# Wider spill rows, one fetch per half stack, and score maxima dealt from the third quad on

## What is computed

```
x   = x + layernorm(attention(layernorm(x)))       # q, k, v = x @ W.T + b, 16 heads
x   = x + layernorm(ffn(layernorm(x)))
ffn: xn = norm(x); abel = gelu(xn @ abel_w + b); top 2 of xn @ moe_gate_w
     moe = sum of the two experts, then three rotations; out = x + abel*(1-gate) + moe*gate
```

## Time and profile before

| | |
|---|---|
| median of 3 runs | 1971.94 us (1971.53 to 1973.84) |
| the profiled execution: its time | 1979.73 us |
| the profiled execution: its span | 1977.9 us |
| mean granted TensorE clock | 0.942 |
| PE busy | 1598.2 us, 81% |
| DVE busy | 1217.5 us, 62% |
| ACT busy | 930.2 us, 47% |
| POOL busy | 706.5 us, 36% |
| DMA moved | 241.47 MB, mean 122 GB/s |

### The profile page before, as it was taken

The page is one execution under the profiler, slowest core; times in us unless marked ns, Lnnn a source line. Parts: engine busy times, 40 slices in busy tenths (PEclk is TensorE's granted clock), DMA queues, the critical chain, the costliest instruction groups (busy, mean ns, idle before and its releaser), DMA issues. The chain is left out here.

```text
span 1977.9 us, 33425 instructions
## 1 busy us (share of the span) xinstructions
PE 1598.2 (81%) x10429; PEld 1074.0 (54%) x10430; DVE 1217.5 (62%) x3633; ACT 930.2 (47%) x1788; POOL 706.5 (36%) x716
## 2 busy tenths in 40 slices
PE   3888887888888888888888888849999999999800
PEld 2544444444444444444444444538888888888700
DVE  6756675675775775775765765334565566556367
ACT  1045655755755755755755646412332333233234
POOL 1011223423423423423413413522444444444458
PEclk9899999999999999999999998979999999999955
DMA  3233234234234234234144132574565565565377
GB/s 118 80 108 97 67 108 148 74 121 151 73 124 149 70 124 151 72 123 150 68 127 140 60 121 69 165 219 107 124 140 123 114 143 126 108 140 118 45 264 252
DMA packets 185548, 241.47 MB, mean 122 GB/s; under 512 B 24585, under 2 KB 156049, under 8 KB 185297
## 3 DMA queue, kind: packets, MB, share of 16 engines
q1 hardware_dynamic: 158544, 203.58, 32.6%
q0 software_dynamic: 26880, 36.33, 11.1%
HBM read 133.40 MB, written 105.91 MB: 121 GB/s over the span
## 5 line engine op out<-in xcount | busy, mean ns | idle before, releaser
L952 ACT ACTIVATE pexp<-scT 128x512 f32<-128x512 f32 x768 | 441.8, 601 | 355.1 <-PE scT L739 343.8
L1122 DVE TENSOR_REDUCE mx<-work 128x1 f32<-128x320 f32 (+2 forms) x1024 | 492.8, 549 | 50.6 <-PE work L719 47.7
L1599 POOL DMA_INDIRECT y_rows<-rows_add,row_of x144 | 227.0, 1576 | 295.6 <-DMA y_rows<-rows_add,row_of 225.3
L739 PE MATMUL scT<-w 128*128 128x192 bf16 (+3 forms) x1536 | 275.6, 278 | 54.8 <-ACT pexp L952 53.8
L719 PE MATMUL work<-w 126*128 126x320 bf16 (+4 forms) x1280 | 265.8, 300 | 55.4 <-DVE mx L1122 25.9
L1631 PE MATMUL h_ps<-inT,w1c 128*128 128x256 f32 x1152 | 263.1, 382 | 2.4 <-DVE inT L1683 2.4
L1644 PE MATMUL o_ps<-w,hT 128*128 x1152 | 260.4, 379 | 0.0
L1631 PEld LDWEIGHTS h_ps<-inT,w1c 128*128 128x128 f32 x1152 | 220.4, 192 | 33.5 <-issue 2.9
L739 PEld LDWEIGHTS scT<-w 128*128 128x128 bf16 x1536 | 124.3, 98 | 205.4 <-ACT pexp L952 142.0
L1574 ACT ACTIVATE rows_add<-rows_out,row_share 128x257 f32<-128x257 f32 x144 | 65.9, 506 | 354.6 <-DVE rows_out L1699 266.1
L1644 PEld LDWEIGHTS o_ps<-w,hT 128*128 128x128 f32 x1152 | 213.4, 190 | 26.1
(11 more groups left out here) (173 smaller groups left out, 2176.0 us busy)
## 6 DMA issues: line engine op xcount, KB each, us to landing
w<-split_spill SPq DMA_DIRECT2D x384, 128.0 KB, 3.0
split_spill<-split SPq DMA_DIRECT2D x64, 384.0 KB, 3.2
rows_in<-z_rows SPq DMA_DIRECT2D x72, 265.0 KB, 5.4
y_rows<-pre SPq DMA_DIRECT2D x16, 514.0 KB
y<-y_rows SPq DMA_DIRECT2D x16, 514.0 KB, 6.7
x_rows<-x SPq DMA_DIRECT2D x16, 512.0 KB, 2.6
abel_rows<-pre SPq DMA_DIRECT2D x16, 512.0 KB
abel_in<-abel_rows SPq DMA_DIRECT2D x16, 512.0 KB
```

The source lines that it names most:

```text
L739: ins = nc.tensor.matmul(scT[n % 2][:, at:at + hi - lo], tile(kst[par][0:K_EXP, h, :], t), qst[par][0:K_EXP, h, lo:hi], start=True, stop=True)
L952: nc.scalar.activation(pexp[:, (q * GROUP + n) % NPB, :], scT[n % 2][:, :], ACT.Exp, scale=DH ** -0.5).then_inc(s_exp, 1)
L1122: nc.vector.reduce_max(mx[:, c:c + 1], work[t][:, 0:n], AX_X).then_inc(w_free[t], 1)
L1599: pool.indirect_dma_start(kept.y_rows, bass.IndirectOffsetOnAxis(ap=row_of[n][:, r:r + 1], axis=0), rows_add[n % 2][:, r, :], None, comput ...
```

## The change

The spill gets six slots for each projection in place of three, in the order of the products. `put` issues three DMAs, of three, two and one slot (768 KB in all where it was 384 KB); for k, a part is repeated by a broadcast source. The products are reordered so that this works; they are the same six pairs. `restack` is one DMA of 96 partitions (768 KB) where it was six of 16. On SP `put(2)` comes before `restack(0)`, and the load of x comes behind all fetches, no longer ahead of the first `put`. The maxima go in two DMAs where they went in eight, for which their column is now h * 4 + t. `B_FROM` is 2: the 64 max units go over ten quads, six or seven a quad. On DVE both `values` come ahead of `finish_a(2)`, no longer behind `finish_a(3)`.

```diff
-Q_PART = [0, 0, 1, 1, 0, 2]
-K_PART = [0, 1, 0, 1, 2, 0]
-NGRP = len(Q_PART)
+PRODUCTS = [(0, (0, 1, 2), (0, 0, 0)), (3, (0, 1), (1, 1)), (5, (0,), (2,))]
+NGRP = 6
-B_FROM = 3
+B_FROM = 2
-        spill = nc.dram_tensor("split_spill", [2, 4, P, 3, S], BF16, kind="Internal").ap()
+        spill = nc.dram_tensor("split_spill", [2, 4, P, NGRP, S], BF16, kind="Internal").ap()
...
             def put(b, par, m):
                 sp.wait_ge(s_split, b * 4 + m + 1)
-                sp.dma_start(spill[par, m], split[:, m, :, :]).then_inc(s_spill[m], 16)
+                for at, q_parts, k_parts in PRODUCTS:
+                    n = len(q_parts)
+                    if m % 2:
+                        src = split[:, m, k_parts[0]:k_parts[0] + 1, :].broadcast_to([P, n, S])
+                    else:
+                        src = split[:, m, 0:n, :]
+                    sp.dma_start(spill[par, m][:, at:at + n, :], src).then_inc(s_spill[m], 16)
 
             def restack(b, par, m):
                 half = m // 2
-                st, parts = (kst, K_PART) if m % 2 else (qst, Q_PART)
-                sp.wait_ge(s_spill[m], b * 16 + 16)
-                for g, part in enumerate(parts):
-                    src = spill[par, m].rearrange("(h d) s c -> d h s c", d=DH)[:, :, part, :]
-                    sp.dma_start(st[par][g:MASK_ROW:NGRP, 8 * half:8 * half + 8, :], src)\
-                      .then_inc(s_stack[half], 16)
+                st = kst if m % 2 else qst
+                sp.wait_ge(s_spill[m], (b + 1) * len(PRODUCTS) * 16)
+                src = spill[par, m].rearrange("(h d) g c -> (d g) h c", d=DH)
+                sp.dma_start(st[par][0:MASK_ROW, 8 * half:8 * half + 8, :], src).then_inc(s_stack[half], 16)
...
             def step(s, par, i):
                 if here(s, 0):
-                    if not isinstance(s, int) or s + 2 < B:
-                        sp.wait_ge(s_bn, (s + 1) * NTOK)
-                        sp.wait_ge(s_xn, (s + 1) * NTOK)
-                        plain(sp)
-                        load_x(sp, xin[par], s + 2, s_xin[par])
                     wait(sp, s_sc, (s - 1) * UNITS)
...
                     put(s, par, 0)
                     put(s, par, 1)
+                    put(s, par, 2)
                     restack(s, par, 0)
-                    put(s, par, 2)
-                    restack(s, par, 1)
                     put(s, par, 3)
-                    restack(s, par, 2)
-                    restack(s, par, 3)
+                    for m in range(1, 4):
+                        restack(s, par, m)
+                    if s + 2 < B:
+                        sp.wait_ge(s_bn, (s + 1) * NTOK)
+                        sp.wait_ge(s_xn, (s + 1) * NTOK)
+                        plain(sp)
+                        load_x(sp, xin[par], s + 2, s_xin[par])
...
-                    for t in range(NT):
-                        for part in range(N_MAX):
-                            r = MAX_ROW + part
-                            sp.dma_start(qst[par][r:r + 1, :, t * P:(t + 1) * P],
-                                         mrow[t * HEADS:(t + 1) * HEADS, part, :]).then_inc(s_mrow, 16)
+                    for part in range(N_MAX):
+                        r = MAX_ROW + part
+                        sp.dma_start(qst[par][r:r + 1, :, :].rearrange("o h (t c) -> o (h t) c", c=P),
+                                     mrow[:, part, :]).then_inc(s_mrow, 16)
...
             def maximum(b, h, t):
-                c = t * HEADS + h
+                c = h * NT + t
...
(DVE, step)
+                if proj:
+                    for n in range(2):
+                        values(s, par, n)
                 if finish:
                     finish_a(s - 2, 2)
                 more = not isinstance(s, int) or s + 1 < B
                 if more:
                     stats(s + 1, 1 - par)
                 if finish:
                     finish_a(s - 2, 3)
-                if proj:
-                    for n in range(2):
-                        values(s, par, n)
```

More of the change, by code:

```diff
@@ L713, in max_unit @@
                 if t == 0 and h % 8 == 0:
-                    pe.wait_ge(s_stack[h // 8], (b + 1) * 2 * NGRP * 16)
+                    pe.wait_ge(s_stack[h // 8], (b + 1) * 2 * 16)
                 use(b, t, ("max", h))
@@ L735, in score_unit @@
                 if q == 0 and n == 0:
-                    pe.wait_ge(s_mrow, (b + 1) * NT * N_MAX * 16)
+                    pe.wait_ge(s_mrow, (b + 1) * N_MAX * 16)
                 wait(pe, s_exp, u - 1)
@@ L916, in first_part @@
                 full(act, b, w, "project")
-                wait(act, s_spill[m], b * 16)
+                wait(act, s_spill[m], b * len(PRODUCTS) * 16)
                 nc.scalar.activation(split[:, m, 0, :], work[w][:, :], ACT.Identity,
@@ L927, in first_max @@
                 full(act, b, 0, "turn")
-                wait(act, s_mrow, b * NT * N_MAX * 16)
+                wait(act, s_mrow, b * N_MAX * 16)
                 nc.scalar.copy(mrow[:, 0, :], work[0][0:NT * HEADS, 0:P]).then_inc(s_m1, 1)
```

## The result

The changed kernel takes 2110.39 us (median of four runs, 2109.65 to 2112.88) against 1972.89 for the kernel before beside it: ratio 1.0685, interval 1.0642 to 1.0727. It is slower, as forecast, but by 138 us and not by 25; the range ended at 2026. The profiled execution took 2110.36 us with a span of 2108.5, 130.6 longer than before. In what follows one execution of w1_sp_order (8909 us) and one of v7_dense_early_shifts_behind (4137 us) stood far apart from the others of their kernels, and their times and ratios leave them out.

A forecast was written before the change was run, and what follows sets the result against it. PE and DVE, neither full, wait for each other at the maxima. Terms +1.2, +1.3, -1.2 give +1.3 us a full step, +17 for thirteen; with +2 for step 0 and +3 each for steps 1, 2: +25, 1997 us, range 1950 to 2026.

The forecast's parts named there:

- the prediction's own sign: Stated test for the DMA rate: it is wrong if the stack takes other than 15.8 us from the first put.
- Start of DVE's maxima: Full step, DVE: PE waits for the stack, so the shifts before the first maximum come later: +1.2 us.
- When the low half lands: Stack's low half, step 8: 4.72 MB at 358 GB/s plus 2.6 us fixed; lands at 627.7, 0.5 us late.
- My lower end: Slow bound for the stack's landing: 273 GB/s, at 631.8, 4.6 us late.
- Dense behind maxima: Full step after DVE's first maximum: `dense` waits for max units and DVE idles for `dense`: +1.3 us.
- The hand layout: DVE's idle time from its first maximum to the end of `route`, laid out by hand: 3.4 us, before 2.1.
- (c): Rival, chance 0.11: transfers near 300 GB/s, stack 3.0 to 4.1 us late, and a cold PE; 2030 us.
- Fewer units a quad: Quads 3 to 11 have 6.4 units each where they had 7.1: -1.2 us a full step, between 0 and -4.
- SP's queue: SP's DMA issues: 18 fewer, 12 us of SP a step, costed at nothing.
- (b): Rival, chance 0.26: more even shares close DVE's idle time; -2 us a step, 1946, or 1956 us.
- (a): Rival, chance 0.15: transfers at 390 GB/s bring the stack in time, +0.6 us a step; 1982 us.

The follow-up runs named there:

- w1_sp_order: t2_orders with SP's order of the changed kernel (load of x behind all fetches, put 2 ahead of restack 0): ratio 1.0419 to the kernel before, 2066 us.
- v7_dense_early_shifts_behind: u3_before_dense_early with DVE's two shifts moved behind the third quad's work: ratio 0.9941 to the kernel before.
- t2_orders: Kernel before, its transfers kept, with `B_FROM` = 2 and both `values` ahead of `finish_a(2)`: ratio 1.0361, 2054 us.
- w2_warm_both: Changed kernel with the score units at both PE waits of the third quad issued twelve times over, same output: ratio 1.0531 to the kernel before.
- u6_six_fetches: Changed kernel, doubled spill kept, with each quarter stack fetched in six transfers of 16 partitions: ratio 1.0670 to the kernel before.
- t1_transfers: Changed kernel with only its transfer edits: `B_FROM` back at 3 and `values` late as before: ratio 1.0050 to the kernel before, 1990 us.
- t3_values: Kernel before with only the `values` moved ahead of `finish_a(2)`: ratio 1.0014.
- v6_all_early: Kernel before with `B_FROM` = 2, `values` early, shifts behind third-quad maxima, `dense` pairs a quad earlier, `turn_ctx(3)` ahead of first max units: ratio 0.9874, 1957 us.
- u3_before_dense_early: Kernel before with the two pairs of `dense` behind the second and third quad, not the third and fourth: ratio 0.9945, 1968 us.

## Why the prediction was wrong in size

The direction and the place came as written: the first max unit waits for the DMA, the shifts come later, the fifth unit waits for DVE with the clock down behind it, `dense` waits for maxima. The sizes did not: the wait of about a microsecond is 3.8, the step longer by 1.3 us is longer by 9.25, and the rate is wrong by the prediction's own sign, since the stack does not take 15.8 us. Two terms failed by a factor, and a third left out work that the change moves. Measured over full steps:

- **Start of DVE's maxima, +1.2 us. Measured +4.6** (shifts 28.06 us into a step before, 32.70 after). In t2_orders, where the stack comes as before, it is +0.55. The first step that failed is "When the low half lands". I took the 358 GB/s of a stretch of spills for the fetches too and called it the rate of back-to-back transfers. Spills did better than that, 394 GB/s, and fetches in a full queue 223 to 230. With these, four spills take 8.0 us and two fetches 6.9, and with 2.6 fixed that is 17.5; from the first third part to the first max unit it was 18.15 in the mean, where I had 15.9 (it was 17.1 to 17.3 in four steps, and 19.8 in one). My lower end laid 273 GB/s on spills and fetches alike and came to 20.0. The wait it makes is 3.8 us in the mean. PE's cold clock behind this wait adds 1.7 on the way to `turn_ctx(3)`, by the 3.96 us of the changed kernel against the 2.29 of w2_warm_both. Something goes the other way, which the prediction did not see: the first third part ends 7.54 us into a full step and not 8.43, since in eight of the thirteen full steps before PE began the step at about half clock (603.00 to 606.00 in step 8: 0.50), and in none after.
- **Dense behind maxima, +1.3 us. Measured +3.4.** From DVE's first maximum to the end of the second pair of `dense` it is 6.0 us before, with seven maxima in it, and 12.7 after, with twelve and two `pre` more. DVE is idle for 2.1 us of it before and for 5.5 after. The hand layout (2.1 and 3.4) had the waits in the right places and at the wrong clock: in the six steps of w2_warm_both in which the pair ran at full clock it is 3.3 us. The second step that failed is that this cold clock is in no term. The prediction named it, and put it into rival (c) as an addition, although the nearly 3 us of idle PE that bring it were in the forecast itself, longer than the idle time behind which the earlier trace rows show it. w2_warm_both prices it at 3.4 us or more a full step over both terms.
- **Fewer units a quad, -1.2 us. Measured +1.25.** Behind `dense` a step now has 52 units for DVE and not 57, 2.4 us less work, and this part became 1.15 us shorter (39.30 to 38.15). As a length that is what the term foretold. But the 2.4 us of the five units now stand ahead, between the first maximum and the end of the second pair, and the sum has them nowhere: its term for `dense` counts DVE's idle time alone. Counted as idle time too, this term is +1.25: half of the work taken away came back as idle time. The "6.0 to 8.8 us of DVE a step" are no room that work can fill at will; PE's order decides when it can.

These give 4.6 + 3.4 + 1.25 = 9.25 us, which is the measured 9.25; the sum had +1.3. The clock's share of the second term is shown by w2_warm_both; the part of the rate in the first is read from the trace, since no run changed the rate alone. Step 0 came to +1.0 (+2 foretold), steps 1 and 2 to +5.8 and +10.4 (+3 each). SP's queue at nothing was right (u6_six_fetches, t1_transfers) but for the 0.3 us of delay by its order (w1_sp_order), and so were the `values` nearly (t3_values).

Of the rivals, (c) had the mechanism: fetches at a lower rate and a cold PE. Its price, 3.7 us a step, was under half of the truth, because it left the clock out of its sum. (b) had a true core that it could not show in this change: a full step of v6_all_early is 2.25 us shorter than before, near the 2 of (b), once what stood between DVE and its units is gone. That the two numbers meet is luck in part, since 1.1 of it came in u3_before_dense_early with the maxima left where they were. The formula of the Trainium skill ("DMA: Bandwidth & Descriptors", "Anatomy of one DMA") gave, as an estimate, a landing 12.8 us after the first put; the page fits it to DMAs issued from GpSimd, and here SP issues them. The trace disagrees, with 18.15 us from the first third part to the first max unit, and (a) falls with it. The advice of the same page of the Trainium skill ("Rules for kernel authors") to coalesce small transfers found nothing to gain here, by u6_six_fetches.

What stays open is why fetches in a full queue move 223 to 230 GB/s where spills move 394. The trace of the changed kernel rules two answers out. The third number from the end is again the clock, the last the GB/s:

```profile
685.50:687.00 1.50, 1.50 (x13) 0.60 (x13) 0.00 (x0) 0.10 (x1) 0.00 (x0) 0.98 1.09 384
...
1433.00:1436.00 3.00, 2.23 (x16) 1.68 (x15) 1.13 (x8) 1.34 (x3) 0.00 (x0) 1.00 1.05 406
```

At 685.5 to 687 the queue spills a k projection, whose repeated part goes out in pieces of 1 KB like those of the fetches, at 384 GB/s: small pieces alone are not the reason. At 1433 to 1436, behind the last full step, it loads weights from HBM in pieces of 2 KB, at 406 GB/s: the direction alone is not either. The loads of x behind the fetches, in pieces of 1 KB too, moved 255 GB/s (698.2 to 701). What is left is small pieces and the direction together, the span of memory that a fetch reads, and its 96 partitions where a spill has 128; no run here took these apart.

## What to carry to other kernels

Before work is dealt earlier, write down for each engine of the pair what stands in its own program ahead of the first piece. Four buffers full in front of an engine that waits for a third engine are worth nothing, and what the producer has behind the fifth is then late too. An idle time that a hand layout predicts for TensorE is to be followed by the cold clock that the trace shows behind idle times of that length, in the forecast and not in a rival. A sum of work and idle time needs both in every part: work that is moved earlier is booked there, not only taken off where it was. And a rate is to be taken from a stretch with the same kind of transfer, direction and pieces alike, not from the best one near it.

## What was not expected of the hardware

- Score units repeated in PE's waits kept the granted clock at 1.00 in step 8 through what had been idle time; a kernel with some 5 us more work a step ran 3.4 us a step faster (w2_warm_both), though the clock still fell in seven of thirteen full steps.
- With the queue full, spills of SBUF to HBM moved 394 GB/s and the fetches back 223 to 230, each with the share of the DMA engines at or over 1. Fetched in six parts, paced by SP at 0.64 us for 131 KB, the same bytes moved 208 GB/s with a share of 0.69.
- The same queue moved 384 GB/s of spills in pieces of 1 KB and 406 GB/s of loads in pieces of 2 KB, so neither the piece nor the direction makes the fetches slow by itself.
